# Adding the squared deviations of four subsets on GpSimd, so that TensorE averages one sum in place of four

## What is computed

```python
v  = group_norm(x, 32 groups of 16 channels, eps=1e-5)     # per image and group: mean and variance
xg = v.reshape(B, 4, 128, H, W) rotated by one conv group
xa = round(clip((xg - lA) / (uA - lA), 0, 1) * 15) / 15     # 16 levels
wq = (round(clip((w - lW) / (uW - lW), 0, 1) * 15) / 15 - 0.5) * 2
y  = einsum('bgihw,goi->bgohw', xa, wq)                     # four 128 x 128 products, 1x1 convolution
y  = relu(y * inv + (beta - running_mean * inv)) + v        # inv = gamma / sqrt(running_var + eps)
out = x + y
```

## Time and profile before

| | us |
|---|---|
| median of 3 runs | 258.81 (258.80 to 259.05) |
| profiled execution | 258.41 |
| its span in the trace | 256.7 |
| VectorE busy | 230.0 (90%) |
| ScalarE busy | 215.2 (84%) |
| GpSimd busy | 212.0 (83%) |
| TensorE busy | 193.9 (76%) |
| moved by DMA | 103.25 MB, mean 402 GB/s |

### The profile page before, as it was taken

One profiled execution on the slowest core, in us unless ns is written; L12 is line 12 of the kernel. 1 busy time (PEld: TensorE's weight loads), 2 busy tenths in 40 slices (PEclk: granted clock), 3 DMA queues, 4 the chain that ended last, 5 costly groups with the idle time before them and its releaser, 6 DMA issues.

```text
span 256.7 us, 3463 instructions
## 1 busy us (share of the span) xinstructions
PE 193.9 (76%) x999; PEld 109.3 (43%) x999; DVE 230.0 (90%) x363; ACT 215.2 (84%) x394; POOL 212.0 (83%) x340
## 2 busy tenths in 40 slices
PE   1142996969889888979797997877696969889920
PEld 0132644435454444445443554343444435454510
DVE  2898698999999999999999899999999999969940
ACT  4437898999999999989999889999899888999300
POOL 6126869999999999999999999999999999999100
PEclk9999999797979798988979599999979797979995
DMA  6999999999999999999999999999999999999994
GB/s 225 398 411 411 408 409 406 418 416 417 418 414 418 417 416 418 411 418 416 416 415 416 418 416 413 419 417 415 417 413 418 416 418 409 402 400 402 393 399 193
DMA packets 34516, 103.25 MB, mean 402 GB/s; under 512 B 1202, under 2 KB 1730, under 8 KB 34498
## 3 DMA queue, kind: packets, MB, share of 16 engines
q1 hardware_dynamic: 18624, 54.86, 53.8%
q10 hardware_dynamic: 15874, 48.18, 47.0%
HBM read 51.65 MB, written 51.38 MB: 401 GB/s over the span
## 4 chain that ended last, share of the span: by engine, by line
POOL 52%; DVE 16%; issue 11%; PE 9%; ACT 5%; DMA 2%; DVEq 0%; SPq 0%; POOLq 0%; ACTq 0%
POOL images L413 27%; POOL levels L424 8%; DVE images L482 7%; PE prod L604 6%; DVE stats L460 4%; POOL dev L375 3%; DVE codes L475 3%; PE var_ps L584 3%; POOL dev L378 2%; DMA images<-in_x 2%; POOL scaled L404 2%; ACT levels L270 2%; POOL coef L406 2%; POOL norm L402 1%; ACT unused L242 1%
## 5 line engine op out<-in xcount | busy, mean ns | idle before, releaser
L604 PE MATMUL prod<-codes,w_t 128*128 128x392 bf16 x768 | 160.8, 369 | 7.9 <-DVE codes L475 2.9
L482 DVE SCALAR_TENSOR_TENSOR images<-prod,floor,images 128x784 f32<-128x784 f32 x128 | 128.0, 1019 | 8.5 <-PE prod L604 8.2
L413 POOL TENSOR_SCALAR images<-images,coef 128x784 f32<-128x784 f32 x120 | 123.7, 1042 | 0.0
L604 PEld LDWEIGHTS prod<-codes,w_t 128*128 128x128 bf16 x768 | 79.1, 110 | 81.6 <-issue 24.6
L270 ACT ACTIVATE levels<-images,coef 128x784 int16<-128x784 f32 x95 | 91.3, 1028 | 1.1 <-issue 1.1
L460 DVE BATCH_NORM_STATS2 stats<-images 128x6 f32<-128x392 f32 x136 | 68.9, 551 | 5.4 <-DMA images<-in_x 5.4
L236 ACT ACTIVATE unused<-images 128x784 bf16<-128x784 f32 x60 | 50.7, 847 | 7.5 <-DMA images<-in_x 5.2
L242 ACT ACTIVATE unused<-images,sums 128x784 bf16<-128x784 f32 x60 | 56.1, 939 | 0.1
L475 DVE TENSOR_SCALAR codes<-levels 128x3136 bf16<-128x3136 int16 x32 | 34.7, 1085 | 1.0 <-ACT levels L270 0.7
L584 PE MATMUL var_ps<-dev,avg 128*128 128x8 f32 x128 | 19.6, 280 | 20.0 <-POOL dev L382 20.0
L424 POOL TENSOR_SCALAR levels<-images,coef 128x784 int16<-128x784 f32 x33 | 33.6, 1020 | 0.1
(11 more groups left out here) (66 smaller groups left out, 83.2 us busy)
## 6 DMA issues: line engine op xcount, KB each, us to landing
images<-in_x SPq DMA_DIRECT2D x30, 1568.0 KB, 14.5
out<-images ACTq DMA_DIRECT2D x30, 1568.0 KB, 18.8
images<-in_x SPq DMA_DIRECT2D x8, 392.0 KB, 6.6
out<-images SPq DMA_DIRECT2D x1, 1568.0 KB, 8.8
out<-images SPq DMA_DIRECT2D x4, 392.0 KB, 7.4
w_raw<-in_weight SPq DMA_DIRECT2D x1, 256.0 KB, 6.5
rows<-in_channel_params ACTq DMA_DIRECT2D x1, 8.0 KB, 2.3
limit_row<-in_limits ACTq DMA_DIRECT2D x1, 0.0 KB
```

The lines of the kernel that those rows point to most:

```text
L413: nc.gpsimd.tensor_scalar(here, here, coef[:, u % 2, 0, 1, G * j + o:G * j + o + 1], coef[:, u % 2, 1, 1, G * j + o:G * j + o + 1], ALU.mu ...
L482: nc.vector.scalar_tensor_tensor(out=two, in0=prod[:, k % SETS, :, 0:HALF], scalar=floor[:, o:o + 1], in1=two, op0=ALU.max, op1=ALU.add).t ...
L604: done = nc.tensor.matmul(prod[:, k % SETS, h, 0:HALF], w_t[:, part, output_group(g)], codes[:, n % 2, g, h * HALF:(h + 1) * HALF], start= ...
```

## The change

GpSimd's squares are written as 8 x 4 numbers. Two more instructions add the four subsets: first halves (columns 0 and 1 to columns 2 and 3, 16 results), then those two (8 results). Each waits for the one before it by the semaphore dev_step, which now counts three steps per pair. TensorE then makes one product from the 8 sums where it made four, one for each subset. The matrix avg is the same. Four products of four numbers or one product of their sum give the same average up to rounding.

```diff
-        dev2 = sb("dev2", [P, 2, G, SUBSETS], F32)
+        dev2 = sb("dev2", [P, 2 * G, SUBSETS], F32)
+        dev2_half = sb("dev2_half", [P, 2 * G, SUBSETS // 2], F32)
+        dev2_sum = sb("dev2_sum", [P, 2 * G], F32)
...
+            FOLDS = 3
+
+            def folded(u, k, ins):
+                ins.then_inc(dev_step, 1)
+                pool.wait_ge(dev_step, FOLDS * u + k)
+
             def deviations(u):
...
-                nc.gpsimd.tensor_tensor(dev[:, :, k:G], own[:, :, k:G].to_broadcast([P, 2, G - k, SUBSETS]),
-                                        mean[:, :, k:G].to_broadcast([P, 2, G - k, SUBSETS]),
-                                        ALU.subtract).then_inc(dev_step, 1)
-                pool.wait_ge(dev_step, u + 1)
-                nc.gpsimd.tensor_tensor(dev2[:], dev[:], dev[:], ALU.mult).then_inc(dev_done, 1)
+                folded(u, 1, nc.gpsimd.tensor_tensor(dev[:, :, k:G], own[:, :, k:G].to_broadcast([P, 2, G - k, SUBSETS]),
+                                                     mean[:, :, k:G].to_broadcast([P, 2, G - k, SUBSETS]), ALU.subtract))
+                dev_ = dev[:].rearrange("p j g s -> p (j g) s")
+                folded(u, 2, nc.gpsimd.tensor_tensor(dev2[:], dev_, dev_, ALU.mult))
+                folded(u, 3, nc.gpsimd.tensor_tensor(dev2_half[:], dev2[:, :, 0:2], dev2[:, :, 2:4], ALU.add))
+                nc.gpsimd.tensor_tensor(dev2_sum[:], dev2_half[:, :, 0], dev2_half[:, :, 1], ALU.add).then_inc(dev_done, 1)
...
             def average_deviations(u):
                 pe.wait_ge(dev_done, u + 1)
-                var = var_ps[:, 0:2 * G].rearrange("p (j g) -> p j g", g=G)
-                for s in range(SUBSETS):
-                    done = nc.tensor.matmul(var, avg[:], dev2[:, :, :, s], start=False, stop=(s == SUBSETS - 1))
-                done.then_inc(var_done, 1)
+                nc.tensor.matmul(var_ps[:, 0:2 * G], avg[:], dev2_sum[:], start=False, stop=True).then_inc(var_done, 1)
```

## The result

The changed kernel takes 260.24 us (median of 22 runs, 258.37 to 261.38); the kernel before, run beside it, 258.72 us (22 runs, 258.23 to 260.19). The ratio of the two is 1.004, 95% interval 1.0025 to 1.0055; a second series of 9 runs gave 259.87 us and 1.0043 (1.0028 to 1.0057). So it is slower by 1.0 to 1.5 us, where +2.6 was forecast. The direction and the range held; the forecast size was 1.7 to 2.6 times the measured one.

What follows compares the result with a forecast made beforehand. Transfers were taken to bound the kernel, with GpSimd pacing compute: 7.4 - 1.4 - 0.7 - 0.2 = 5.1 us later, less slack 2.5, +2.6, so 261.4 us with the offset to the median; range 258.7 to 263.6.

Steps and rivals of the forecast that it cites:

- What bounds the kernel: Whole run: transfers are the limit, with compute seen only where it leaves them without work; packed GpSimd paces compute.
- The price per pair: GpSimd, from squares to affines: two sums with their waits make 0.79 us of 0.22, +0.57 per pair.
- The locks: Port pair shared by GpSimd and VectorE: 0.78 us lost per codes instruction, with no stall added for the sums.
- The start: Pairs 0 and 1, where GpSimd waits for the average: fewer passes give -1.4 us, bounds -0.9 and -1.9.
- The waits filled: GpSimd from 36 to 240 us: the new work fills its idle waits, -0.7 us.
- pair 15: Last pair, path from 225.33 through the average to VectorE's end: +0.57 - 0.80 = -0.2 us.
- The slack: End of the store queue: images 30 and 31 may come 2.5 us later at no cost, bounds 2.2 to 3.1.
- The offset to the median: From profiled execution to median: 0.4 us added, taking 261.0 to 261.4 us.
- The signs: In the changed trace: period 14.5 us, first codes 0.5 to 2 earlier, last store near 252, landing sooner, GB/s dip.
- Hidden entirely: End of the store queue: it covers all 5.1 us of later compute, time 258.8 us; chance 0.17.
- Compute gets faster: Whole run: sums fit GpSimd's free time, some 4 us off the path, transfers leave 0.2, 258.6 us; chance 0.05.
- The whole shift is paid: Sums cost the upper bound or worse, start gives nothing back: +5.9 us, 264.7 us; chance 0.10.

Runs made afterwards that it cites:

- Start only: Changed kernel with sums and single product in pairs 0 and 1 alone, old form in the other 14; 258.75 us, ratio 0.9998 to the kernel before.
- one product: Kernel before with one TensorE product, from subset 0 alone, in place of four, GpSimd as before; 258.44 us, ratio 0.9981.
- half of the sums: Changed kernel with only the sum of 16 on GpSimd and two products on TensorE; 258.56 us, ratio 0.9989 to the kernel before.
- sums only: Kernel before plus GpSimd's two sums, used by nobody; TensorE keeps its four products; 262.17 us, ratio 1.0141.
- four more instructions: Kernel before with four unused GpSimd instructions of 8 elements added per pair, without waits; 264.83 us, ratio 1.0215.
- lighter kernel before: Kernel before, storing only two of four groups of images 12 to 27; 256.76 us, ratio 0.9921.
- second one before: A further profiled execution of the kernel before, unchanged; store of image 30 issued at 244.22, span 257.06 us.
- one more instruction: Kernel before with one unused GpSimd instruction of 8 elements added per pair, without a wait; 258.71 us, ratio 0.9989.
- lighter changed kernel: Changed kernel, storing only two of four groups of images 12 to 27; 259.66 us, ratio 1.0027 to the kernel before.

## Why the prediction was right in direction and wrong in size

**What bounds the kernel: right.** Both halves stand. Transfers set the end of the kernel before: with a quarter of the stores left out it is 2.0 us shorter, and the changed kernel only 0.2 to 0.6. (Start only, one product and half of the sums don't show it, since compute ended no earlier or later in them.) GpSimd sets the pace of compute (sums only, four more instructions).

**The price per pair: right.** +0.57 was worked out; the trace shows 0.80 in place of 0.22, and the period went from 13.96 to 14.55 as forecast (14.5).

**The locks: right in number.** They still cost GpSimd one block of 0.78 per codes instruction and no more for the two sums. What I did not foresee is that VectorE pays more as well: 32 codes instructions take 37.9 us in place of 34.7. The period grew by no more than GpSimd's own 0.58, so nothing of it is seen there.

**The start: the forecast -1.4, measured -1.9,** the bound; pair 2 starts at 40.29 in place of 42.18. ScalarE did not hold it at 0.9.

**The waits filled, and pair 15:** GpSimd's 0.7 us of waits are gone, as forecast, but the 13 periods from pair 2 to pair 15 grew by 7.3 us in all, where 7.4 - 0.7 = 6.7 was forecast. That makes up for the start, by luck. From pair 15 to the store of image 30 the stretch is 19.01 us against 19.13: -0.1 for -0.2. In sum the store of image 30 comes 5.27 us later where 5.1 was forecast, between these two executions; for others see below.

**The slack: this is the step that failed.** "Less the slack of 2.5" took too little off, for the execution that the sum was made on. The term was 2.5 us, from "if nothing were queued ahead, images 30 and 31 would be out at 243.2 + 2.3 + 8.0", 10.3 us after the issue; with the 0.7 from the last landing to the span's end that makes 11.0. Four executions of the changed kernel, whose queue has run empty, take 10.1. So the slack of the execution that I summed is 3.4, and the forecast for the span was 0.9 too long, less 0.2 for the shift: 259.3 forecast, 258.59 measured. The 2.3 us of an 8 KB transfer from the first microsecond was not the price of a store at the end: that of image 30 lands 5.4 us after its issue, of which 4.0 are the data at 400 GB/s, leaving 1.4. The bounds that I gave the slack, 2.2 to 3.1, left that out. The 1.4 is no constant: the same store took 6.2 us in sums only, 5.9 with four more instructions and 5.8 in the lighter kernel before, which leaves 2.2, 1.9 and 1.8, and these kernels end 10.9, 10.6 and 10.5 us after the issue. Why the changed kernel's stores land sooner is open. By the kernels with more GpSimd work in the old form the slack would have been 2.6 to 2.9, inside my bounds.

**The offset to the median: a second, smaller slip.** I carried the 0.4 us between the profiled execution of before and its median over to the changed kernel, whose profiled execution, 260.32, lies at its median. 0.9 - 0.2 + 0.4 + 0.1 is the 1.2 us between 261.4 and 260.24.

**One execution taken for the kernel.** Slack and offset go wrong together because the sum was made on one execution, and an early one. An estimate from the times: a run of the lighter kernel before, whose end compute sets, lasts 1.7 + 10.5 us beyond its store of image 30, so its 11 runs (255.40 to 258.49) issue that store between 243.2 and 246.3, with 244.6 in the median. By the same working, with 1.7 + 10.1, the changed kernel's 22 runs issue it between 246.6 and 249.6, 248.4 in the median. So in the median the change makes compute some 3.8 us later, not 5.1, and the slack is 258.72 - 1.7 - 10.1 - 244.6 = 2.3. Seen from 243.19 the shift was right and the slack short by 0.9; seen from a typical execution the slack was nearly right and the shift 1.3 too long. Either way 1.5 us remain and not 2.6. The profiled executions agree: the four of the changed kernel come 3.3 to 4.3 us after the second one before, and the lighter pair is 3.7 apart. The estimate takes it that leaving stores out does not change compute's own pace; pair 15 starts at 224.77 there and at 224.67 in the second execution before.

**The baseline.** The ratio (1.0 us) is lower than the medians (1.5) because the times of the changed kernel are spread to the low side: 8 of 22 runs lie at 258.4 to 259.5, 14 from 260.0 up. The four profiled executions lie between 259.4 and 260.4, and the mean granted clock of the 22 runs doesn't sort them (258.37, 258.44 and 261.38 us all at 0.90), so what was shorter in the shortest ones is open.

**The signs.** The period of 14.5, the last store at 252.4 landing 5.5 us later and the dips in GB/s (from 236 us on) all came. The first codes instruction starts only 0.1 us earlier, the second 1.9 (31.69 for 33.58).

**The rivals.** "Hidden entirely" is what happens to smaller doses (one more instruction, half of the sums), by their times; its point of decision, 2.5 to 3.1 us, was too low for the execution it was made for (3.4). "Compute gets faster" is refuted from a side that I had not worked out: not only do queued stores hold the end, the loads hold compute (one product). "The whole shift is paid" did not occur even with four more instructions, which paid 6.7 of 9.6 us in the profiled execution.

## What to carry to other kernels

When transfers and one engine are close to each other as limits, a change is to be costed twice: the shift of compute on its pacer, and the point from which that shift is seen. The first could be taken from start-to-start distances of neighbouring instructions: 0.57 us per pair worked out, 0.56 to 0.58 measured. The second needs the time from the last large issue to the end with an empty queue, which here varied from 10.1 to 10.9 us between kernels, and it needs more than one execution, since compute's end varies by some 3 us from run to run (the estimate above) where the transfers hide it. A saving on an engine with idle time in every period (here six passes of TensorE) is worth nothing there, while its price on the packed engine is paid in every period: put such work where the period has room, or leave it.

## What the runs showed of the hardware that I had not expected

The stretch from pair 15's deviations to VectorE's last instruction holds nearly the same work in each kernel, and its length goes with TensorE's granted clock in it, with one exception. Windows of it in the kernel with half of the sums, in the changed kernel and in the one with four more instructions (us, busy of PE, PEld, DVE, ACT, POOL, then PEclk, DMA share, GB/s):

```profile
225.42:246.86 21.44, 17.91 (x105) 9.50 (x102) 21.33 (x24) 14.73 (x18) 14.31 (x22) 1.00 1.03 400
```

```profile
229.45:252.20 22.75, 18.35 (x98) 9.90 (x98) 21.05 (x23) 13.50 (x17) 14.57 (x23) 0.92 0.85 334
```

```profile
231.67:256.56 24.89, 20.80 (x104) 11.49 (x104) 21.54 (x23) 14.02 (x17) 14.79 (x25) 0.86 0.75 296
```

Over all fourteen profiled executions: 21.4 to 21.7 us at 1.00 (half of the sums, one more instruction, sums only), 22.7 to 23.5 at 0.92 or 0.93 (eight executions, both kernels among them), 23.7 and 24.9 at 0.86 (the lighter changed kernel, four more instructions). Here 1.00 is the 2.4 GHz level throughout, and the others are part of the time at 1.2 GHz. The cleanest pair is the kernel before, 22.9 at 0.93, and the same with one more GpSimd instruction, 21.6 at 1.00. The exception is one product, 21.4 at 0.92, so the mean alone does not decide it. Which of the two is the cause, the clock or something that moves both, is not shown.

In a kernel that transfers bound, such differences are not seen; the changed kernel has lost that cover. Its 22 runs spread over 3.0 us against 2.0 for the kernel before, and the lighter kernel before, which has no cover either, spreads over 3.1. That the clock makes this spread is not shown: the changed kernel's four profiled executions all took 22.7 us at 0.92.

The DMA engines of the kernel before fade out over the last four microseconds (304, 166, 53 and 9 GB/s from 252 to 256 us, one microsecond each); in the changed kernel, whose queue had run empty three times in the last 20 us, they move 411 GB/s from 256 to 257 and 113 in the next, and are done.
